# Attention scores in 64-row halves of a channel chunk: spread keys half as wide, heads in another order

## The reference, cut to what matters

```
q, k, v = (xm @ Wqkv) per head           # 16 heads, head dim 16
scores = einsum('bhqd,bhkd->bhqk', q, k) * hd**-0.5
scores = causal mask (layer 2) or key padding mask (layer 0)
attn = softmax(scores); out = einsum('bhqk,bhkd->bhqd', attn, v)
x = x + gate * (out @ Wproj + b);  x = x + gate * mlp(norm(x))
```

## Time and profile before

| what | value |
|---|---|
| median of three executions | 4727.68 us (4727.61 to 4728.84) |
| the profiled execution, its span | 4730.7 us |
| busy PE / PE weight load | 94% / 79% |
| busy DVE / ACT / POOL | 88% / 87% / 85% |
| attention layer 0, blocks 0 to 3 | from about 23 us to about 269 us |
| attention layer 2, blocks 0 to 3 | from about 1769 us to about 2025 us |
| one steady block | about 60.6 us |
| score matmuls (L1147) | 32 pairs of sequences, 256 records, 592 ns median |
| spread keys (L2405) | 128 instructions, 172.7 us busy |

### The profile page before, as it was taken

How to read it: one execution, slowest core, us unless ns; L and a number is a source line. 1 busy time by engine, 2 the same in 40 slices (tenths; PEclk the granted TensorE clock), 3 DMA queues, 4 the chain that set the end, 5 groups by cost and what they waited for, 6 DMA issues and landing times.

```text
span 4730.7 us, 83542 instructions
## 1 busy us (share of the span) xinstructions
PE 4447.0 (94%) x32940; PEld 3726.9 (79%) x32940; DVE 4158.6 (88%) x4037; ACT 4125.1 (87%) x6871; POOL 4003.5 (85%) x1078
## 2 busy tenths in 40 slices
PE   8989899899899998999999999999999999999998
PEld 4458788788778884458888888888888888888887
DVE  6668989989989986759999998999998998999996
ACT  3559899899899974569999999999999999999996
POOL 4439899889889984448999998999998999989996
PEclk8999999999999999999999999999999999999999
DMA  3001111111111121011121211211211211211111
GB/s 124 1 15 51 50 46 51 45 46 47 49 45 47 55 68 38 1 39 55 54 76 54 75 54 50 76 59 54 76 54 48 78 59 57 73 50 60 59 59 41
DMA packets 90085, 252.74 MB, mean 53 GB/s; under 512 B 12240, under 2 KB 26448, under 8 KB 89696
## 3 DMA queue, kind: packets, MB, share of 16 engines
q1 hardware_dynamic: 89696, 247.40, 15.3%
HBM read 243.70 MB, written 3.67 MB: 52 GB/s over the span
## 4 chain that ended last, share of the span: by engine, by line
PE 50%; ACT 23%; POOL 12%; DVE 9%; issue 7%; DMA 0%; DVEq 0%; SPq 0%; POOLq 0%; ACTq 0%
PE psum L1015 13%; PE psum L1001 10%; PE psum L748 9%; PE psum L998 7%; ACT weights_c L1546 7%; POOL work L2372 6%; PE psum L1115 5%; ACT work L1546 4%; ACT weights_c L1561 4%; ACT work L1561 4%; POOL weights_c L2372 4%; DVE work L1992 4%; DVE weights_c L1992 2%; PE psum L1191 2%; ACT L1316 1%
## 5 line engine op out<-in xcount | busy, mean ns | idle before, releaser
L2372 POOL TENSOR_TENSOR work<-work,weights_a 128x2048 f32<-128x2048 f32 x512 | 2333.3, 4581 | 238.9 <-DVE work L1992 236.7
L1992 DVE TENSOR_TENSOR_SCAN work<-weights_c,psum 128x512 f32<-128x512 f32 x1366 | 1572.0, 1202 | 112.8 <-PE psum L1001 105.3
L1015 PE MATMUL psum<-ident,work 128*128 128x128 f32 x8192 | 1242.6, 275 | 22.8 <-POOL work L2372 22.6
L2372 POOL TENSOR_TENSOR weights_c<-weights_c,weights_a 128x2048 f32<-128x2048 f32 x256 | 1168.5, 4584 | 73.1 <-DVE weights_c L1992 72.2
L1546 ACT ACTIVATE work<-work,decay 128x504 f32<-128x504 f32 x1366 | 964.6, 706 | 55.8 <-DVE weights_c L1992 25.8
L1015 PEld LDWEIGHTS psum<-ident,work 128*128 128x128 f32 x8192 | 969.3, 143 | 34.5 <-POOL work L2372 33.4
L1001 PE MATMUL psum<-ident,work 128*128 128x128 f32 x5464 | 938.5, 274 | 0.0
L1992 DVE TENSOR_TENSOR_SCAN work<-work,psum 128x512 f32<-128x512 f32 x682 | 791.0, 1202 | 43.1 <-PE psum L1001 33.6
L1992 DVE TENSOR_TENSOR_SCAN weights_c<-work,psum 128x512 f32<-128x512 f32 x684 | 792.5, 1202 | 38.7 <-PE psum L1001 33.7
L1001 PE MATMUL psum<-ident,weights_c 128*128 128x128 f32 x3752 | 697.3, 276 | 0.0
L1001 PEld LDWEIGHTS psum<-ident,work 128*128 128x128 f32 x5464 | 672.9, 143 | 0.0
(11 more groups left out here) (201 smaller groups left out, 6500.6 us busy)
## 6 DMA issues: line engine op xcount, KB each, us to landing
weights_a<-c_rows SPq DMA_DIRECT2D x384, 512.0 KB, 3.6
weights_c<-in_L_cond_fwd_in_w SPq DMA_DIRECT2D x8, 512.0 KB, 7.6
weights_c<-in_L_cond_fwd_xproj_w SPq DMA_DIRECT2D x4, 1024.0 KB, 7.7
weights_c<-in_L_cond_bwd_in_w SPq DMA_DIRECT2D x8, 512.0 KB, 5.9
weights_c<-in_L_cond_bwd_xproj_w SPq DMA_DIRECT2D x4, 1024.0 KB, 7.9
x_stream<-in_x_t SPq DMA_DIRECT2D x4, 512.0 KB, 8.7
weights_a<-in_L_cond_w SPq DMA_DIRECT2D x2, 1024.0 KB, 15.0
weights_a<-in_L_cond_W SPq DMA_DIRECT2D x2, 1024.0 KB, 8.0
```

What stands on the lines that cost most here:

```text
L1015: last = nc.tensor.matmul(PS[:, t, j * P:(j + 1) * P], buf["ring"][s % RING][:, j, t * P:(t + 1) * P], IDENT[:, :], start=begins, stop=((s ...
L1992: v.tensor_tensor_scan(buf["ring"][s % RING][:, j, along], buf["decay"][q % DECAYS][:, along], PS[:, 4 + q % LOOKAHEAD, along], 0.0, ALU.mult,
L2372: g.tensor_tensor(state, state, buf["c"][:, s // 2 % 2, s % 2, :].unsqueeze(1).broadcast_to([P, DC, T]), ALU.mult).then_inc(ss["prod_ready ...
```

## The change

The contraction of a score runs over one head's 16 channels, and the spread keys are zero elsewhere. A chunk's 128 rows are now taken as two halves g = 0, 1 of 64 rows, each with four heads. A score matmul has 64 rows by 64 columns, 256 moving columns, an explicit tile position (64g, 64r), and writes bank g, columns 256c to 256c+255. So there are eight matmuls for a pair where there were four. Spread keys are 128 x 256 per instruction instead of 128 x 512; both halves of the partitions hold their own four heads in the same columns. HMASK's columns 4 to 7 are added into columns 0 to 3 once, on GpSimd, ahead of the clearing of VBD in layer 0. In S the heads now stand in the order (half, chunk, head); `attend` reads PT through `made_as`. The number and sizes of all other instructions stay as they are.

```diff
-        KBD = region(WORK, 3072, 2, KC, 2, HPC * SEQ)
+        KBD = region(WORK, 3072, 2, KC, 2, HPC // 2 * SEQ)
...
                     def score(p):
-                        for c in range(KC):
-                            claim(c, by("dve", f"seen{p}"))
+                        for bank in range(2):
+                            claim(bank, by("dve", f"seen{p}"))
                         made("pool", f"kbd{p}@{i}")
+                        half = HPC // 2 * SEQ
                         for c in range(KC):
                             for r in range(2):
                                 o = (2 * p + r) * SEQ
-                                last = nc.tensor.matmul(
-                                    PS[64 * r:64 * r + 64, c, :], Q[:, c, o:o + SEQ],
-                                    KBD[:, p % 2, c, r, :], start=True, stop=True)
+                                for g in range(2):
+                                    rows = slice(64 * g, 64 * g + 64)
+                                    last = nc.tensor.matmul(
+                                        PS[64 * r:64 * r + 64, g, c * half:(c + 1) * half], Q[rows, c, o:o + SEQ],
+                                        KBD[rows, p % 2, c, r, :], start=True, stop=True,
+                                        tile_position=(64 * g, 64 * r))
...
                         for h in range(HEADS // 2):
                             q4 = 32 * (h % 4)
+                            made_as = h // 2 % 2 * 4 + h // 4 * 2 + h % 2
...
-                                    PT[:, p % 2, h, r * SEQ:(r + 1) * SEQ], start=True, stop=True,
+                                    PT[:, p % 2, made_as, r * SEQ:(r + 1) * SEQ], start=True, stop=True,
...
                 if l == 0:
                     pool.wait_ge(dma_small, 16 * 2)
+                    g.tensor_tensor(HMASK[:, 0:HPC // 2], HMASK[:, 0:HPC // 2], HMASK[:, HPC // 2:HPC], ALU.add)
+                    pool.drain()
...
-                                    KF[:, c, o:o + SEQ].unsqueeze(1).broadcast_to([P, HPC, SEQ]),
-                                    HMASK[:, :].unsqueeze(2).broadcast_to([P, HPC, SEQ]), ALU.mult)
+                                    KF[:, c, o:o + SEQ].unsqueeze(1).broadcast_to([P, HPC // 2, SEQ]),
+                                    HMASK[:, 0:HPC // 2].unsqueeze(2).broadcast_to([P, HPC // 2, SEQ]), ALU.mult)
```

## The result

The change makes the kernel faster by a little: 4717.65 us (4713.73 to 4723.64, 11 executions) against 4727.68 us (4726.37 to 4729.71, 11 executions) before; the ratio is 0.9981, with a 95% interval of 0.9973 to 0.9989. A second set gave 4717.53 against 4728.34 us, ratio 0.9974 (0.9964 to 0.9984). So some 10 to 11 us are gained where 15.2 were forecast. The kernel before's own median lies between 4727.68 and 4730.49 us in four sets of executions, so the experiments are to be compared by their ratios, each taken within one set. The span of the profiled execution went from 4730.7 to 4717.0 us.

The account below looks back on a forecast made before the run. TensorE was taken to bound steady blocks (59.7 of 60.6 us busy), with VectorE's chain as tight. Gains of 12.6 (six steady blocks) + 2.3 + 0.3 (blocks 0) = 15.2 us gave 4712.5 us; range 4704 to 4726.

Parts of the forecast that it names:

- rival 2: Score row halves run only partly beside each other, 1.4 us a pair; 9.7 us gained, 4718 us; chance 0.10.
- rival 1: Score row halves do not run beside each other, a pair stays at 1.72 us; 3.5 us gained, 4724; chance 0.11.
- rival 3: VectorE gains nothing, its slow work not being due to the spreads; 5.5 us gained, 4722 us; chance 0.08.
- Scores: TensorE's score pairs: 16 records run four at a time, 0.86 us a pair instead of 1.72.
- rival 4: Slower: a pair's 16 score records go one after another, 3.44 us; 44 us lost, 4772 us; chance 0.07.
- Score 0: First score of a block: gives TensorE 0.7 us, less than the others' 0.86, because shape changes around it are new.
- Spread keys: GpSimd's spread instructions, 256 elements instead of 512: 0.61 us each instead of 1.04, bounds 0.52 and 1.04.
- VectorE's lead: In a steady block, VectorE's work beside shorter spreads gets cheaper: 1.5 us earlier at exp 0, 2.2 at norm 1.
- up3: Up product needing gelu0: TensorE reaches it at 109.0 us, gelu0 is done at 108.7, so just free.
- attend 0: TensorE step waiting for ScalarE's copy, limiting its lead to 2.0 us; 2.1 us taken for each of six steady blocks.
- Block 0 of layer 0: VectorE leads there and TensorE waits for norm 1; fewer delays beside spreads gain 2.3 us, bounds 0.9 and 3.
- The rest: Outside the blocks: mask addition hidden on GpSimd, else a fraction of a microsecond; the scan layers only start earlier.

Follow-up runs that it names:

- rows_same: The whole change, but both products of a pair of halves read rows 0 to 63, two tiles instead of four; 4734.95 us, one execution.
- keys_wide: The kernel before with only the scores in halves, spread keys left 512 wide; 4727.95 us, ratio 0.9996.
- downs_more: The whole change plus down products cut otherwise, score 0 ahead of v0 and up5 ahead of attend 0; 4704.17 us, ratio 0.9953.
- keys_narrow: The kernel before with only the spread keys halved to 256 wide, each 128-row score product reading them twice; 4727.43 us, ratio 0.9996.

## Why the prediction was right, and where it was off

The time lies in the range and on the side forecast; the forecast was 4712.5. The time alone would not have shown the mechanism: 4717.65 is the price of rival 2 (4718), and the range was wide enough for rivals 1 to 3. The rows of the pairs and of VectorE decide.

- *Scores.* 0.86 us a pair between equal shapes was taken; 1.02 us with the changes of shape was measured, as given for score 1. Rivals 1, 2 and 4 (1.72, 1.4 and 3.44 us) are out. In `rows_same` twice the weight loads cost 0.05 us a pair, so rival 4's reason is out too.
- *Score 0.* The forecast gave it 0.7 us, the rows give 0.49. The prediction read 0.15 us as the price of two changes of shape (1.87 against 1.72 us from a score's start to the next start). That distance holds only the change behind the score; the one ahead lies in the distance before it: v0 to score 0 took 1.80 us before and takes 1.95 now. So two changes cost some 0.3 us, and this term was mis-sized by 0.2 us a block.
- *Spread keys.* 0.61 us taken, 0.614 measured.
- *VectorE's lead.* 1.5 us forecast at exp 0, 2.2 at norm 1. Norm 1 now ends 34.41 us after k0 instead of 37.36, so it leads by 2.95: I had left the subtraction of pair 1 and next_normed at their old cost, and they fell from 1.70 and 2.06 to 1.26 and 1.63 us. The forecast wait of 0.8 to 1 us ahead of turn 1 did not come, and TensorE waits 0.65 us ahead of turn 2 instead; a wait ahead of turn 1 appeared in `keys_wide`, where this lead is missing, and in `downs_more`, where TensorE's is larger.
- *up3.* Forecast as just free with both halves and as waiting without VectorE's lead: the second is the 0.66 us of `keys_wide`. Rival 3, VectorE gains nothing, is out; `keys_wide` is the kernel as rival 3 saw it.
- *attend 0.* Forecast as the step that limits, through the copy whose chain starts at up3's end: so it was. The copy's chain has up3's lead, 1.34 us, and the copy was ready 0.38 us early before the change; that makes 1.72 us where I had 1.6 + 0.4. The block ends with this 1.72 (1.76 in layer 2), not 2.1. Times six that is 10.5 us, not 12.6.
- *Block 0 of layer 0.* 2.3 us forecast, 2.8 measured up to turn 1. *Block 0 of layer 2*: 0.3 forecast, not to be told from its 1.6 us of variation.
- *The rest.* The terms of the forecast, as measured, sum to 10.5 + 2.8 = 13.3 us, while the medians moved by 10.0 and 10.8. That the spans moved by 13.5 (mean of two against mean of two) is no check of this sum: whole block 0 gave 5.4 us in that mean, the fifth turn took 3.7 back, and the other stretches happened to make up the difference. The sentence that failed is that what lies behind the blocks only starts earlier, and one of the prediction's own signs of being wrong came true, the blocks short and a stretch outside longer. The fifth turn of layer 0 got 5.7 and 1.7 us longer at a lower granted clock. It was longer than before's 60.2 us in all ten traces of other kernels (61.4 to 66.0), also in `keys_narrow` and `rows_same`, whose steady blocks are as full as before's, so the new waits in the blocks are not needed for it. That the clock does it is shown by the windows; why the kernel before keeps 1.00 there twice is open, and so is where the 3 us between the medians and this sum went. Two traces of a kernel are too few for a stretch that varies by 4 or 5 us.

How far the two engines hold each other up can be read off now. The Trainium skill's page "SBUF — State Buffer", section "Who interferes with whom", says that a VectorE instruction with two inputs in SBUF contends with a GpSimd instruction that reads SBUF, and that the contention is an exclusive lock. The trace agrees: next_normed's excess over 1.22 us was 0.84 beside spreads of 1.04 us and is 0.41 beside spreads of 0.61 us, in both cases 0.2 us less than the length of one spread; row maxima, with one input, took 1.20 to 1.22 us beside them in every kernel.

The prediction left at 0.15 us for two what the page "TensorEngine Tiling (Array Packing)" of the Trainium skill, section "Tiling Modes", calls a drain at each change of mode. The trace agrees that each change costs: 0.15 us ahead of score 0 (1.95 against 1.80 us) and 0.15 us behind a score before the change (1.87 against 1.72). The 1.02 us of a pair now is 0.16 more than the 0.86 us estimated for four tiles at a time.

## What to carry to other kernels

When an engine is at 98% in a stretch, look for the second chain that is as tight: here half of the change alone gave 0.0 or 0.4 to 0.6 us a block, both together 1.7. After the change read the new waits of the full engine and see whether work that stands behind them can be put ahead; here cutting sixteen products at other places gave as much again (1.7 us a block) as the change itself. Where GpSimd and VectorE work beside each other, a shorter GpSimd instruction can pay twice: here it also took some 0.4 us off VectorE's two-input work beside it.

## What the runs showed of the hardware

Four tiles of 64 by 64 ran beside each other in float32. From the up products, 0.44 us for 512 columns, a record of 256 columns is estimated at 0.22 us, so 16 of them at 3.5 us one after another; they took 1.02 us with the change of shape behind them, and 1.92 us on two tiles. The steady blocks agree to 0.02 us between two traces of one kernel; stretches where TensorE waits more and longer differ by up to 5 us, with the granted clock: block 0 of layer 0 took 56.3 us in one trace at a mean of 0.85 and 61.3 us in another at 0.75, its clock falling to 0.50 (1.2 GHz) at different moments.
